# A graph message-passing kernel: receiver one-hots made one pair earlier, and a residual moved behind the edge loop

## The reference, cut to what matters

```python
def _painn_block(x, edge_index, edge_attr1, edge_attr2, ...):
    ...
    v_msg = v_j * s1[:, :, None] + s3[:, :, None] * edge_attr1[:, None, :]
    msg = jnp.concatenate([v_msg.reshape(E, 384), s2], axis=1)
    x = x + jax.ops.segment_sum(msg, dst, num_segments=N_NODES)
    ...
    msg = jnp.concatenate([v.reshape(E, 384), scal], axis=1)
    x = x + jax.ops.segment_sum(msg, dst, num_segments=N_NODES)
    return x
...
x = _layernorm(x + _L0_gnn_ref(x, edge_index, ...), axis=-1)
```

## Time and profile before

| what | value |
|---|---|
| median of three runs | 520.19 us (517.67 to 526.25) |
| span of the profiled execution (its page gives no other time of its own) | 519.7 us |
| first gather issued | 35.65 us |
| last gather issued | 448.30 us |
| stores of the last group issued | from 457.88 us |
| sums of blocks 8 and 9 read | from 462.48 us |
| PE transposes x1 of block 8 | 466.30 us |

### The profile page before, as it was taken

How to read it: one execution, slowest core, us unless ns; L and a number is a source line. 1 busy time by engine, 2 the same in 40 slices (tenths; PEclk the granted TensorE clock), 3 DMA queues, 4 the chain that set the end, 5 groups by cost and what they waited for, 6 DMA issues and landing times.

```text
span 519.7 us, 14474 instructions
## 1 busy us (share of the span) xinstructions
PE 455.2 (88%) x5181; PEld 289.5 (56%) x5181; DVE 446.5 (86%) x773; ACT 445.6 (86%) x841; POOL 354.6 (68%) x376
## 2 busy tenths in 40 slices
PE   4948788879998998989979998898998898889995
PEld 3434445446654655655645565465565565568783
DVE  6789899999999999999999999999998988821192
ACT  3549998988999999899999999899999989958452
POOL 8837777777777777777777777777777777830200
PEclk9976999999999999999999999999999999999998
DMA  8797888888888888888888988888888888610022
GB/s 236 263 346 236 264 254 265 268 273 260 269 274 254 272 277 273 261 264 255 251 252 277 283 266 270 257 272 262 256 255 249 289 257 257 211 47 1 3 103 101
DMA packets 46687, 123.18 MB, mean 237 GB/s; under 512 B 9441, under 2 KB 22309, under 8 KB 46605
## 3 DMA queue, kind: packets, MB, share of 16 engines
q0 software_dynamic: 25120, 102.91, 63.9%
q1 hardware_dynamic: 17245, 13.33, 8.3%
q10 hardware_dynamic: 4240, 5.90, 3.4%
HBM read 110.11 MB, written 12.00 MB: 235 GB/s over the span
## 4 chain that ended last, share of the span: by engine, by line
POOL 32%; PE 25%; issue 15%; DVE 12%; DMA 11%; ACT 2%; DVEq 0%; SPq 0%; ACTq 0%; POOLq 0%
POOL side L604 24%; POOL work L604 9%; DMA side<-node_table,src_c 8%; PE psum L1563 7%; DVE side L1133 4%; PE psum L1454 3%; PE psum L1416 3%; DVE side L1130 2%; PE psum L1428 2%; PE psum L1448 2%; PE psum L1349 2%; DMA w<-in_L_gnn_W 1%; PE psum L1474 1%; PE psum L1492 1%; DMA node_table<-work 1%
## 5 line engine op out<-in xcount | busy, mean ns | idle before, releaser
L604 POOL DMA_INDIRECT side<-node_table,src_c x234 | 233.6, 998 | 71.3 <-issue 67.7
L743 ACT ACTIVATE side<-key_no,less_key 128x320 bf16<-128x320 f32 x314 | 160.6, 566 | 0.4
L752 ACT ACTIVATE scratch<-side,one_f 128x640 bf16<-128x640 bf16 x157 | 129.5, 825 | 0.0
L1448 PE MATMUL psum<-side,scratch 128*32 128x512 f32 x468 | 123.1, 605 | 1.2 <-DVE side L1133 1.2
L1133 DVE TENSOR_TENSOR side<-side,psum 128x768 f32<-128x768 f32 x117 | 110.6, 945 | 0.0
L604 POOL DMA_INDIRECT work<-node_table,src_c x80 | 84.6, 1058 | 31.5 <-issue 29.3
L1416 PE MATMUL psum<-w2s,scratch 128*128 128x384 bf16 x314 | 79.1, 335 | 28.2 <-DVE side L1133 22.5
L1454 PE MATMUL psum<-side,scratch 128*32 128x128 f32 x1404 | 98.4, 275 | 0.0
L1130 DVE TENSOR_TENSOR side<-side,psum 128x512 f32<-128x512 f32 x117 | 79.6, 680 | 15.1 <-DMA side<-node_table,src_c 14.8
L1454 PEld LDWEIGHTS psum<-side,scratch 128*32 128x32 f32 x1404 | 71.1, 109 | 0.0
L1428 PE MATMUL psum<-scratch 128*128 128x320 bf16 x314 | 65.4, 318 | 0.0
(11 more groups left out here) (224 smaller groups left out, 781.9 us busy)
## 6 DMA issues: line engine op xcount, KB each, us to landing
side<-node_table,src_c POOLq DMA_INDIRECT x234
sum_rows<-stage SPq DMA_DIRECT2D x208, 16.0 KB
sum_rows<-zeros_bf SPq DMA_DIRECT2D x3, 896.0 KB, 8.2
node_table<-work ACTq DMA_DIRECT2D x8, 320.0 KB, 5.0
scratch<-sum_rows SPq DMA_DIRECT2D x10, 256.0 KB, 4.3
out<-xw SPq DMA_DIRECT2D x9, 256.0 KB
xw<-in_x ACTq DMA_DIRECT2D x2, 768.0 KB, 11.7
work<-node_table,src_c POOLq DMA_INDIRECT x80
```

Source lines behind the costliest of these rows:

```text
L604: g.indirect_dma_start(out=rows[i % SLOT_PAIRS][:, j, :], out_offset=None, in_=node_table, in_offset=bass.IndirectOffsetOnAxis(ap=src_c[:, ...
L743: a.activation(key_off[:, b, j, :], key_no[:, :], ACT.Abs, bias=less_key[:, t:t + 1]).then_inc(L["key_off_made"], 1)
L752: a.activation(key_hot[:, n % 2, t:t + 2, :], key_off[:, b, :, :], ACT.Relu, bias=one_f[:, :], scale=-1.0).then_inc(L["key_hot_made"], 1)
L1448: mm(bank[b][j * SPAN:(j + 1) * SPAN, :], hot[:, n % 2, t + j, 0, :], rows[s][:, j, 0:4 * C], start=first, stop=True, skip_group_check=True)
```

## The change

It has two parts.

1. `receiver_hots(n)` makes only the plain one-hots, and is called a pair earlier, right behind `sender_hots` (i % 3 == 1). The attribute product is a function of its own, `attribute_hots(n)`, and stays at i % 3 == 2. The wait for line 1107's result is kept, but a pair of messages now lies between.
2. In the loop, the eight residuals are gone, and `take_v(w)` no longer waits for them. Behind the loop SP reads the sums of blocks 0 to 7 once more, into five buffers `sums_again` laid over slots 0 and 1 of the gathered rows; DVE makes 2*xw + sums with two instructions for each block (three vectors, then scalars). The first five blocks stand ahead of `new_x1(8)` on DVE, the last three behind `new_x1(9)`. On SP the first five reads stand ahead of the wait for the last stores, the last three behind the reads of blocks 8 and 9, and each of those waits for its buffer. Blocks 8 and 9 keep the old form (`late_residual`).

```diff
+AGAIN_BUFS = 5
...
+        r_work.cut(NW * D + 2 * TJ * TW - 2 * 2 * TW)
+        sums_again = [r_work.cut(D) for _ in range(AGAIN_BUFS)]
...
+            sp.wait_ge(L["summed"], max(p for p in range(PAIRS) if p % SLOT_PAIRS < 2) + 1)
+
+            def read_again(w):
+
+                sp.dma_start(sums_again[w % AGAIN_BUFS], block_sums(w)).then_inc(sums_again_in[w % AGAIN_BUFS], 16)
+
+            for w in range(AGAIN_BUFS):
+                read_again(w)
             sp.wait_ge(L["stored"], 64 * LG)
             for w in range(EARLY_BLOCKS, NW):
                 read_sums(w)
+            for w in range(AGAIN_BUFS, EARLY_BLOCKS):
+                sp.wait_ge(S["residual_made"], 2 * (w - AGAIN_BUFS) + 2)
+                read_again(w)
...
                 act.wait_ge(B["v_made"], w + 1)
-                act.wait_ge(B["residual_made"], w + 1)
+                if w >= EARLY_BLOCKS:
+                    act.wait_ge(S["residual_made"], 2 * w + 2)
...
                                 rel_c[:, t].unsqueeze(2).to_broadcast((P, T, SPAN)), ALU.is_equal).then_inc(L["hot_made"], 1)
+
+            def attribute_hots(n):
+                t, b = tiles_of(n), n % 2
+                T = t.stop - t.start
                 dve.wait_ge(L["hot_made"], 2 * n + 1)
...
             def residual(w):
+                sums = sums_again[w % AGAIN_BUFS]
+                dve.wait_ge(sums_again_in[w % AGAIN_BUFS], 16 * (w // AGAIN_BUFS + 1))
+                v.scalar_tensor_tensor(out=xw[:, w, 0:C3].rearrange("p (c k) -> p k c", k=3),
+                                       in0=xw[:, w, 0:C3].rearrange("p (c k) -> p k c", k=3), scalar=2.0,
+                                       in1=sums[:, 0:C3].rearrange("p (k c) -> p k c", k=3), op0=ALU.mult, op1=ALU.add
+                                       ).then_inc(S["residual_made"], 1)
+                v.scalar_tensor_tensor(out=xw[:, w, C3:D], in0=xw[:, w, C3:D], scalar=2.0, in1=sums[:, C3:D],
+                                       op0=ALU.mult, op1=ALU.add).then_inc(S["residual_made"], 1)
+
+            def late_residual(w):
                 dve.wait_ge(B["x1_made"], 2 * w + 2)
-                v.tensor_tensor(xw[:, w, :], xw[:, w, :], kept(x1_new, w), ALU.add).then_inc(B["residual_made"], 1)
+                v.tensor_tensor(xw[:, w, :], xw[:, w, :], kept(x1_new, w), ALU.add).then_inc(S["residual_made"], 2)
...
-            block_steps = [(new_x1, at_slots(0)), (residual, at_slots(1)), (products, at_slots(9)), (dots, at_slots(10)), (update, at_slots(13))]
+            block_steps = [(new_x1, at_slots(0)), (products, at_slots(9)), (dots, at_slots(10)), (update, at_slots(13))]
...
                     if i % GP == 1 and n + 1 < LG:
                         sender_hots(n + 1)
+                        receiver_hots(n + 1)
                     if i % GP == 2 and n + 1 < LG:
-                        receiver_hots(n + 1)
+                        attribute_hots(n + 1)
...
+                for w in range(AGAIN_BUFS):
+                    residual(w)
                 both(new_x1)
-                both(residual)
+                for w in range(AGAIN_BUFS, EARLY_BLOCKS):
+                    residual(w)
+                both(late_residual)
                 both(products)
```

More of the change, by code:

```diff
@@ L270, in build @@
         carry_zeroed pass_done pass_seen pass_begun pass_go bases_read need_set again_ready again_seen again_begun again_go
-        counts_split flags_made flags_summed many_set rest_made update_hi x_again
+        counts_split flags_made flags_summed many_set rest_made update_hi residual_made
         update_split window_done res_made ln_stats ln_mean std_made ln_scale ln_shift y_made y_stored""".split()
@@ L275, in build @@
         table_stored = [sem(f"table_stored{b}") for b in range(TABLES)]
-        block_names = """x1_made residual_made x1T_turned x1T_taken u_made u_taken v_made v_taken v_squared norm_turned norm_made gate_taken z1_made
+        sums_again_in = [sem(f"sums_again_in{b}") for b in range(AGAIN_BUFS)]
+        block_names = """x1_made x1T_turned x1T_taken u_made u_taken v_made v_taken v_squared norm_turned norm_made gate_taken z1_made
         h1_made gate_made prod_made dot_made dot_scaled update_made""".split()
@@ L501, in _ @@
                     sp.sem_clear(done)
-                sp.dma_start(xw[:, 0:NFULL, :], x[0:NFULL * P, :].rearrange("(w p) f -> p w f", p=P)).then_inc(S["x_again"], 16)
-                sp.dma_start(xw[0:NTAIL, NFULL, :], x[NFULL * P:N, :]).then_inc(S["x_again"], 16)
                 sp.sem_inc(S["again_go"], 1)
@@ L1200, in message_pass @@
                 sender_hots(0)
+                attribute_hots(0)
                 for i in range(PAIRS):
@@ L1270, in layer_norm @@
                         dve.wait_ge(S["window_done"], w + 1)
-                        dve.wait_ge(B["residual_made"], w + 1)
+                        dve.wait_ge(S["residual_made"], 2 * w + 2)
                         v.tensor_tensor(res, res, bank[out_bank(w)], ALU.add).then_inc(S["res_made"], 1)
@@ L1316, in _ @@
                 again(dve)
-                dve.wait_ge(S["x_again"], 32)
                 for w in range(EARLY_BLOCKS):
```

## The result

The changed kernel takes 532.02 us, the median of 4 runs (529.79 to 534.65), against 523.0 for the kernel before, measured beside it (4 runs, 517.67 to 526.25): ratio 1.0192, 95% interval 1.0153 to 1.0231. The forecast was 520.9, no change, with a range up to 526.7. It was made from three runs of the kernel before, with a median of 520.19 us; with the fourth the median is 523.0. So what was forecast is +0.7 us, and what was measured is +10.0 by the ratio. The profiled execution is the fastest of the four: 529.79 us, span 527.9, that is 8.2 us over the span before.

A forecast was written before the change was run, and what follows sets the result against it. POOL's issue was taken to bound the loop, PE what lies behind it. From the profiled 519.7 us, -0.2 - 0.6 + 1.5 gave 520.4, and 0.5 to the median gave 520.9 us, range 515.5 to 526.7.

The forecast's parts named there:

- What bounds the kernel: In the loop, POOL's issue of gathers was to be the bound, with DVE close behind; behind the loop, PE.
- DVE bounds the loop: Rival for the loop: DVE is the bound after all, so its freed time counts, giving 510.8 us; chance 0.08.
- Plain one-hots a pair ahead: In the loop, 6.1 us of DVE saved but hidden by POOL; -0.2 us for DVE finishing sooner in the last pairs.
- Residual out of the loop: In the loop, eight instructions fewer, 4.8 us of DVE saved, covered by POOL, so no gain in time.
- Five reads ahead of blocks 8 and 9: Behind the loop, block 8 ready later and PE's transposes late: +1.5 us, bounds +1.1 and +3.1.
- My own signs of being wrong: Behind the loop, PE's stall at the transpose below 0.5 or above 3.5 us; DVE's first residual was expected at about 462.5.
- PE's stall costs its clock: Rival behind the loop: PE's tail runs at the lower clock after the stall, losing 5 us, 526.7 us; chance 0.05.
- What POOL gains or loses by the hold: Gathers held by DVE in the loop: -1.6 without the residual, +1.0 (a fifth of +4.8) for adjoining one-hots; together -0.6 us.
- the hold gets longer: Rival for the loop: adjoining one-hots always hold a gather as one stretch, +4.8 us, giving 526.5 us; chance 0.14.
- The two slow rivals: The longer hold of gathers in the loop (526.5 us, chance 0.14) and PE's lower clock behind it (526.7 us, chance 0.05).

The follow-up runs named there:

- no_attributes: The kernel before without the product of one-hots and edge attributes for 49 of the 52 groups, so partly wrong results; 516.86 us in one run.
- tail_last: The changed kernel with the reads and residuals of the early blocks put behind those of blocks 8 and 9, on SP and DVE; 525.14 us, ratio 1.0069.
- residual_only: The kernel before with the second part of the change alone (residual behind the loop, five reads ahead of blocks 8 and 9); 527.03 us, ratio 1.0114.
- residual_tail_last: The kernel before with the second part alone, but blocks 8 and 9 first on SP and DVE; 520.35 us, ratio 0.9970.
- after_no_branch: The changed kernel with the never-entered block of the second pass, and the branch over it, taken out of SP's program; 524.60 us, ratio 1.0057.
- hots_only: The kernel before with the first part of the change alone (plain one-hots a pair earlier, right behind the sender one-hots); 524.92 us, ratio 1.0051.
- hots_apart: The kernel before with the first part alone, but the plain one-hots ahead of the counts' addition, not directly behind the sender one-hots; 528.42 us, ratio 1.0142.
- both_earlier: The kernel before with plain and attribute one-hots moved together a pair ahead, the wait between them kept; 521.42 us, ratio 0.9977.
- one_place: The kernel before with plain, sender and attribute one-hots directly behind one another at one pair, without waits between them; 532.59 us, ratio 1.0209.
- one_place_gaps: The kernel before with plain, sender and attribute one-hots behind one pair, with a wait between each two; 524.76 us, ratio 1.0050.

## Why the prediction was wrong

**What bounds the kernel: right.** POOL's issue, not DVE, though DVE stood at 94% of a stretch. no_attributes shows it directly, and with it that the rival "DVE bounds the loop" was rightly at 0.08. The freed time went where the forecast said, into waits for gathers (16 to 28 us).

**"Plain one-hots a pair ahead" and "Residual out of the loop": DVE's time, covered as forecast.** The freed time brought the loop nothing. The -0.2 us for DVE finishing sooner is shown by no run.

**"Five reads ahead of blocks 8 and 9": the step that failed, +1.5 forecast, 6.4 to 7.5 us found** (after against tail_last: 1.0192 and 1.0069; residual_only against residual_tail_last: 1.0114 and 0.9970). The wrong part is the start. I read the 2.6 us between SP's last store and its first read as the wait for the stores to land, and concluded that reads which don't need that wait would begin at once. The chain of waits of the kernel before names another cause. Its line 460 is the `sp.If` that became line 464 in the changed kernel:

```profile
459.74 0.05 SPq L460
459.79 2.62 issue
...
462.48 2.68 DMA scratch<-sum_rows
```

By these rows it was the branch then too, and no read placed behind it can begin sooner. No run takes the branch out of the kernel before, so how long SP would have waited for the stores there without it is not known.

How PE's stall became 3.58 us where I had 1.5 can be followed in the rows. The reads came 2.6 us later behind the last store than I had them. From the first read's issue to block 8 ready it took 8.9 us where I had 7.85 (459.75 to 467.6); the 0.78 us for a multiply-add pair was right (464.17 to 464.96 in after_no_branch), and the extra 1.0 is the late third read. Against this, PE itself arrived some 1.4 us later through the low clock at the loop's end. In residual_only, where the clock had not fallen there, the stall is 5.04. My own signs of being wrong had this: a stall above 3.5 us, and DVE's first residual at about 462.5, which came at 467.45.

**"PE's stall costs its clock": wrong chance, and too high a price.** I gave it 0.05, because the stall was to be 1.5 us. The stall was longer and the clock did fall behind it, but the price was not 5 us: it was 1.1 in the changed kernel and 2.0 in residual_only. Most of the loss is PE standing idle (3.58 and 5.04 us). With the clock that makes 4.6 and 7.0 us, which lies within the intervals of the 6.4 and 7.5.

**"What POOL gains or loses by the hold": -0.6 forecast, +3.6 found** (tail_last, 1.0069, in which both parts act in the loop and the tail has no stall; 2.5 to 4.6 by its interval). The -1.6 for the residual held: residual_tail_last gives 0.9970, that is -1.6, with 0 to -3.1 by its interval. The miss is in the one-hots: +1.0 forecast, +2.7 found alone (hots_only, 1.0051), and +5.2 where the residual has left the loop (tail_last against residual_tail_last); the intervals of the two overlap. I had weighed the right mechanism and given it a fifth of its +4.8. What I had not seen is that a gap of 0.03 us between two such instructions, as before line 1110, works for POOL: a gather gets in there. The change put the plain one-hots behind the sender one-hots without such a gap. The rival "the hold gets longer" was right in kind, for the loop. It does not explain all of it in the changed kernel's own profile: of the 3.3 us by which the excess grew, the gathers that end behind a one-hot explain 1.4 (9.9 against 8.5), and the joining as counted above took 1.5 us, against 2.0 and 0.3 in the two profiles of the kernel before. The others lie at the basis and block steps, which the change only shifted in time.

**The sum and the range.** +3.6 for the loop and +6.4 for the order of the reads are the +10.0 measured, with 8.0 to 12.1 by the interval. The two slow rivals stood at 526.5 and 526.7, one at a time, and the range ended there. They do not exclude each other; both at once would have been 531.5 by my own prices, that is +11.3 on the median I started from, where +10.0 was measured, and I had given a time as long as that 0.03. That this comes out so near is in part luck, since my price for the clock was too high and that for the late reads too low.

**What stays open.** Why hots_apart is slow. Why the third read lands late behind the branch. And whether a joined gather is the whole of what the earlier one-hots cost: both_earlier has 3 joined gathers and an excess of 25.1, without being slower.

## What to carry to other kernels

When a share of idle time on a queue is called "issue", look at the line ahead of it before you name its cause: here it was a branch over code that never runs, 2.5 to 2.6 us on the chain, and every read placed behind it inherited them. Ahead of the one transfer that the last engine waits for, nothing else belongs, however cheap its issue. And a short wait between two instructions of an engine that has time to spare is not always waste: where another engine is held by them, the gap is what lets it in, and the same work ran 1.5% faster with two waits more.

## What the runs showed of the hardware

- A taken branch on SP over a block of 45 lines of the kernel was followed by 2.50 us of issue in the changed kernel, 2.62 in the kernel before and 2.75 in residual_only; without the block the next read followed in 0.05. Its price is not in SP's time but in what is queued behind.
- An indirect gather that starts under a DVE tensor_tensor with both inputs in SBUF is nearly always held and ends 0.82 us after that instruction's end. In the kernel before, 63 gathers started with over 0.2 us of such an instruction left, and 57 of them took over 0.99 us; of the 168 that started so under any other DVE instruction, 2 did. If the next such instruction begins 0.1 us before the end of the first, the gather can be held through both; with 0.03 us between them it rarely is (15 joined gathers in one_place, 2 in one_place_gaps). The Trainium skill ("SBUF — State Buffer", Who interferes with whom) has the contention of the two engines; that consecutive instructions can hold a gather as one is shown by these rows alone.
- At the loop's end PE stands idle twice, in the kernel before for 1.16 and 0.79 us. The granted clock was low behind it in half of the 16 profiles without products of zeros (0.67 from 460 to 465 us in the second of the kernel before) and full in the others (1.00 in the first of the same kernel, with the same two waits), so what decides it is not shown.
